# A fused audio tower on one core: idle products at both ends, w_out in four loads, down products that wait by chunk, and new orders of all engines

## The reference, cut to what matters

```
h  = (ln(x @ tok_W.T + tok_b)) * gamma + beta                  # tokenizer
h += attention0(ln(h); w_qkv, w_gates, w_out)                  # 16 heads of 64, softcap 50, causal, gated
h += tanh(ln(h) @ W @ A1 @ A2 + bias)                          # three weights in a row
h += attention1(ln(h); W_qkv, b_qkv, W_proj, b_proj)           # 16 heads of 16, Fenwick mask
h += fp4(silu(fp4(ln(h)) @ fp4(w_gate).T) * (fp4(ln(h)) @ fp4(w_up).T)) @ fp4(w_down).T
```

## Time and profile before

| | |
|---|---|
| three runs | 333.19, 333.32, 334.2 us; median 333.32 |
| the profiled execution | 332.38 us, of which its span is 330.5 us |
| mean granted TensorE clock | 0.974 |
| instructions | 11754, of them 10244 on TensorE (products and weight loads) |
| DMA | 12.80 MB |

### The profile page before, as it was taken

The page is one execution under the profiler, slowest core; times in us unless marked ns, Lnnn a source line. Parts: engine busy times, 40 slices in busy tenths (PEclk is TensorE's granted clock), DMA queues, the critical chain, the costliest instruction groups (busy, mean ns, idle before and its releaser), DMA issues.

```text
span 330.5 us, 11754 instructions
## 1 busy us (share of the span) xinstructions
PE 302.5 (92%) x5122; PEld 266.2 (81%) x5122; DVE 243.9 (74%) x527; ACT 115.5 (35%) x259; POOL 28.7 (9%) x49
## 2 busy tenths in 40 slices
...
GB/s 238 368 344 195 1 3 131 2 2 2 63 4 5 4 2 2 2 3 2 20 3 20 2 4 0 2 4 4 17 3 20 2 2 3 4 2 0 2 0 63
DMA packets 8773, 12.80 MB, mean 39 GB/s; under 512 B 778, under 2 KB 5650, under 8 KB 8724
## 3 DMA queue, kind: packets, MB, share of 16 engines
q1 hardware_dynamic: 8724, 12.06, 11.0%
...
## 4 chain that ended last, share of the span: by engine, by line
PE 85%; DVE 5%; issue 4%; DMA 3%; ACT 1%; SPq 1%; POOLq 0%; POOL 0%; ACTq 0%; DVEq 0%
PE psum L1185 75%; PE psum L1364 2%; PE psum L1386 2%; DMA ffw_raw<-in_L_ffn_aux_weight_dram 2%; PE psum L1490 1%; PE psum L1270 1%; DMA tokw_raw<-in_L_tok_W_dram 1%; PE psum L1245 1%; PE psum L1201 1%; PE psum L1293 1%; ACT hTb L557 1%; DVE hha L820 0%; PE psum L1467 0%; POOLq L220 0%; SPq L472 0%
## 5 line engine op out<-in xcount | busy, mean ns | idle before, releaser
L542 POOL TENSOR_TENSOR ln_rs<-ln_mv,minus_half 128x1 f32<-128x1 f32 x40 | 27.6, 692 | 267.5 <-DVE ln_mv L876 267.5
L1185 PE MATMUL psum<-aT_hi,wqkv_hi 128*128 128x256 f32 x128 | 38.0, 297 | 0.2
L1185 PE MATMUL psum<-aT_lo,wqkv_hi 128*128 128x256 f32 x128 | 36.9, 288 | 0.0
L1185 PE MATMUL psum<-aT_hi,wqkv_lo 128*128 128x256 f32 x128 | 36.6, 286 | 0.0
L557 ACT ACTIVATE qkT<-psum 128x512 f32<-128x512 f32 x32 | 19.1, 598 | 41.8 <-PE psum L1185 41.8
L1185 PE MATMUL psum<-wout_s,oT 128*128 128x256 f32 x128 | 29.2, 381 | 0.0
L1185 PEld LDWEIGHTS psum<-wout_s,oT 128*128 128x128 f32 x128 | 23.9, 190 | 3.3 <-issue 0.2
L1185 PEld LDWEIGHTS psum<-aT_hi,wqkv_hi 128*128 128x128 f32 x128 | 25.0, 196 | 1.2 <-ACT qkT L557 0.3
L1185 PEld LDWEIGHTS psum<-aT_lo,wqkv_hi 128*128 128x128 f32 x128 | 24.9, 195 | 0.1
L1185 PEld LDWEIGHTS psum<-aT_hi,wqkv_lo 128*128 128x128 f32 x128 | 24.9, 195 | 0.0
L1185 PE MATMUL psum<-v_aug,probs 32*32 32x65 f32 x1024 | 19.2, 220 | 0.0
(11 more groups left out here) (222 smaller groups left out, 747.8 us busy)
## 6 DMA issues: line engine op xcount, KB each, us to landing
...
```

Of the source, the lines that this page charges most:

```text
L542: nc.gpsimd.tensor_tensor(ln_rs[:, s, k, j:j + 1], ln_mv[:, s, k, j, 1:2], minus_half[:, :], ALU.pow).then_inc(rstd_ready[f"{k}_{j}"], 1)
L1185: return nc.tensor.matmul(o_, a, b, start=first, stop=last)
```

## The change

1. Ten steps `warm0` to `warm9` in the `pe` list: each waits for the constants and multiplies the identity by 320 columns of the constants into `att` bank 2, where nothing reads it. Two stand ahead of `turn_tok`, one ahead of `xT0.0`, two ahead of `bcast`, five between `tok1.0` and `xT0.1`. Four steps `tail0` to `tail3` do the same into the bank of `out1.3`; one stands ahead of `down_1.3`, three behind it.
2. `wout` loads w_out in four DMAs of 256 KB; ahead of the second to fourth SyncE waits until the one before has landed. `out_` waits for all four.
3. `down` waits for the copy of `hT0` ahead of chunk 0 and for that of `hT1` ahead of chunk 4.
4. All five lists are new.

```diff
@@ sync: wout
             def wout(i):
                 prep.made(sp, 0, "ffwT", "c1T", "ffc")
-                load_w("wout", wout_s[:, :, :], w_out.rearrange("(c p) n -> p c n", p=P))
+
+                n = INNER // P // WOUT_PIECES
+                for k in range(WOUT_PIECES):
+                    if k:
+                        sp.wait_ge(ld["wout"], 16 * k)
+                    load_w("wout", wout_s[:, k * n:(k + 1) * n, :],
+                           w_out[k * n * P:(k + 1) * n * P, :].rearrange("(c p) n -> p c n", p=P))
@@ tensor
+            def warm(i):
+                pe.wait_ge(ld["consts"], 16)
+                mm(att[:, 2, 0:WARM], ident, cst[:, 0:WARM], True, True)
+
+            def tail(i):
+                ring1.read_out(pe, LAST, "out0", "out1")
+                mm(ring1.bank(LAST, "out1")[:, 0:WARM], ident, cst[:, 0:WARM], True, True)
@@ tensor: out_
-                        pe.wait_ge(ld["wout"], 16)
+                        pe.wait_ge(ld["wout"], 16 * WOUT_PIECES)
@@ tensor: down
-                    ring2(i).read_out(pe, i, f"hT0_{j}", f"hT1_{j}")
                     for c in range(FC):
+                        if c in (0, 4):
+                            ring2(i).read_out(pe, i, f"hT{c // 4}_{j}")
```

The starts of the lists, and the end of the `pe` list, before and after (the rest is new in the same way):

```diff
@@ ORDER["pe"], first and last steps
-        turn_tok xT0.0 bcast tok0.0 xT1.0 tok1.0 xT0.1 turn_ff tok0.1 xT1.1 join_ff1 aT.0 tok1.1 qk2.0 qk0.0
-        qk6.0 qk1.0 qk5.0 v02.0 qk7.0 qk3.0 v11.0 v12.0 qk4.0 v01.0 v00.0 v10.0 xT0.2 turn_gate1 aT.1 join_ff2
-        s00.0 s01.0 s10.0 turn_gate0 s11.0 mix00.0 qk7.1 qk3.1 qk5.1 mix01.0 mix02.0 qk4.1 qk0.1 qk6.1 qk1.1
-        mix10.0 v00.1 mix11.0 v02.1 v11.1 oT00.0 mix12.0 oT01.0 v01.1 v10.1 turn_up1 out0.0 turn_up0 v12.1
-        tok0.2 xT1.2 turn_down qk2.1 ...
-        ... u1_0.3 hT0_0.2 hT1_0.2 g0_1.3 g1_1.3 u0_1.3 hT0_1.2 u1_1.3 hT1_1.2 down_0.2 down_1.2 hT0_0.3 hT1_0.3
-        down_0.3 hT0_1.3 hT1_1.3 down_1.3
+        warm1 warm9 turn_tok warm0 xT0.0 warm3 warm6 bcast tok0.0 xT1.0 tok1.0 warm8 warm7 warm2 warm4 warm5
+        xT0.1 turn_ff aT.0 tok0.1 qk7.0 xT1.1 join_ff1 v01.0 v11.0 qk6.0 v10.0 v12.0 qk2.0 qk3.0 v00.0 qk4.0
+        qk5.0 qk0.0 qk1.0 tok1.1 v02.0 turn_gate0 s00.0 s01.0 join_ff2 s10.0 s11.0 mix00.0 turn_gate1 aT.1
+        xT0.2 mix01.0 mix02.0 qk4.1 qk3.1 qk5.1 qk0.1 v02.1 mix10.0 v10.1 qk1.1 qk7.1 qk6.1 qk2.1 oT00.0
+        turn_up0 oT01.0 mix11.0 mix12.0 v11.1 v00.1 v01.1 turn_down out0.0 ...
+        ... hT0_1.2 u1_0.3 hT1_1.2 hT0_0.2 down_1.2 yT_1.3 hT1_0.2 g0_1.3 g1_1.3 u0_1.3 u1_1.3 hT0_0.3 hT1_0.3
+        down_0.2 down_0.3 hT0_1.3 hT1_1.3 tail1 down_1.3 tail3 tail0 tail2
@@ ORDER["act"], first steps
-        turn_tok tables xT0.0 split_qkv1 bcast split_qkv2 xT1.0 split_qkv0 split_qkv4 xT0.1 ...
+        tables turn_tok xT0.0 split_qkv1 bcast xT1.0 split_b split_qkv5 split_qkv3 split_qkv2 xT0.1 split_qkv0
+        aT.0 split_qkv4 turn_ff xT1.1 ...
@@ ORDER["dve"], first and last steps
-        turn_tok xT0.0 split_tokb split_qkv1 tokA0.0 xT1.0 tokB0.0 tokC0.0 split_qkv0 st1_0.0 ln1_0.0 tokA1.0
-        tokB1.0 xT0.1 ... w1b turn_gate1 s0.0 w1c s1.0 turn_gate0 w1d w1e w2a w2b ...
-        ... hh_0.3 hc_1.3 hd_1.3 he_1.3 hf_1.3 hg_1.3 hh_1.3 down_0.2 down_1.2 down_0.3 down_1.3
+        split_tokb turn_tok xT0.0 split_qkv1 tokA0.0 tokB0.0 xT1.0 tokC0.0 st1_0.0 split_b tokA1.0 ln1_0.0
+        tokB1.0 tokC1.0 st1_1.0 split_qkv3 ln1_1.0 xT0.1 split_qkv5 aT.0 tokA0.1 tokB0.1 split_qkv4 xT1.1 w0a
+        ... w2a s0.0 ln1_0.1 turn_gate0 st1_1.1 ln1_1.1 s1.0 w1c aT.1 xT0.2 mixA0.0 w2b mixB0.0 w1d w1e w1f
+        mixC0.0 w2c w1g turn_gate1 w1h w2d w2e w2f w2g turn_up0 w2h mixA1.0 mixB1.0 mixC1.0 out0.0 ...
+        ... sa0_1.3 hh_0.3 sa1_1.3 sb0_1.3 sb1_1.3 ha_1.3 ... hh_1.3 down_0.2 down_0.3 down_1.2 down_1.3
@@ ORDER["sp"]
-        load.2 wout load.3 store_0.0 store_1.0 store_0.1 store_1.1 store_0.2 store_1.2 store_0.3 store_1.3
+        load.2 wout load.3 store_1.0 store_0.0 store_0.1 store_1.1 store_0.2 store_0.3 store_1.2 store_1.3
```

More of the change, by code:

```diff
@@ L35 @@
 SLOTS = 3
+WOUT_PIECES = 4
+WARM = 320
 QKVG = 3 * INNER + H0
@@ L51 @@
[L51 to L65, removed]
@@ L66 @@
-        u1_0.3 hT0_0.2 hT1_0.2 g0_1.3 g1_1.3 u0_1.3 hT0_1.2 u1_1.3 hT1_1.2 down_0.2 down_1.2 hT0_0.3 hT1_0.3
-        down_0.3 hT0_1.3 hT1_1.3 down_1.3""",
-    "act": """
[L69 to L84, removed]
@@ L85 @@
-    "dve": """
-        turn_tok xT0.0 split_tokb split_qkv1 tokA0.0 xT1.0 tokB0.0 tokC0.0 split_qkv0 st1_0.0 ln1_0.0 tokA1.0
[L87 to L110, removed]
-        ya_1.2 sa1_0.2 yb_1.2 sb1_0.2 yc_1.2 yd_1.2 turn1_1.3 ye_1.2 sb0_0.2 yf_1.2 ha_0.2 yg_1.2 den1_0.3
-        yh_1.2 max1_1.3 norm1_0.3 sub1_1.3 yT_1.2 hb_0.2 back1_1.3 hc_0.2 sa0_1.2 proj_0.3 hd_0.2 st4_0.3
-        he_0.2 sa1_1.2 yn_0.3 den1_1.3 ya_0.3 norm1_1.3 hf_0.2 yb_0.3 sb1_1.2 sb0_1.2 yc_0.3 proj_1.3 yd_0.3
-        st4_1.3 ye_0.3 hg_0.2 yf_0.3 yn_1.3 yg_0.3 ya_1.3 yh_0.3 yb_1.3 ha_1.2 yT_0.3 yc_1.3 hb_1.2 yd_1.3
-        hc_1.2 hh_0.2 ye_1.3 hd_1.2 yf_1.3 sa0_0.3 he_1.2 yg_1.3 sa1_0.3 yh_1.3 hf_1.2 sb0_0.3 yT_1.3 hg_1.2
-        sb1_0.3 ha_0.3 hh_1.2 hb_0.3 sa0_1.3 hc_0.3 sb0_1.3 hd_0.3 sa1_1.3 he_0.3 sb1_1.3 hf_0.3 ha_1.3 hg_0.3
-        hb_1.3 hh_0.3 hc_1.3 hd_1.3 he_1.3 hf_1.3 hg_1.3 hh_1.3 down_0.2 down_1.2 down_0.3 down_1.3""",
```

78 lines of the change are left out of this document (71 added, 7 removed).

## The result

| | before | after |
|---|---|---|
| median (lowest to highest), 11 runs each | 333.32 (331.44 to 334.54) us | 329.33 (325.65 to 332.58) us |
| the profiled execution | 332.38 us, span 330.5 | 330.09 us, span 328.2 |
| mean granted TensorE clock in it | 0.974 | 0.984 |

The ratio is 0.9853, with a 95% interval of 0.9811 to 0.9895: 3.5 to 6.3 us faster. It leaves out the changed kernel's three slowest executions (330.68, 330.76 and 332.58 us), which the medians of the table count; by these medians the ratio is 0.988. The two profiled executions differ by only 2.3 us, since the one before lies 0.94 us under its median and the one after 0.76 us over it; terms read from the traces add up to 2.3, not to the 4.0 between the medians.

The account below looks back on a forecast made before the run. From 62 to 282.4 us TensorE's work bounds the kernel, at the end VectorE's chain. 3.9 + 0.6 - 1.0 + 1.0 = 4.5 us off 332.38 gives 327.9, plus 0.94 to the median: 328.8 us, range 323.5 to 332.5.

Parts of the forecast that it names:

- the likeliest case: Whole kernel: the forecast itself holds, 326.5 to 331 us, chance 0.61.
- A: Scores near 53 us: w_out in four loads shortens the stall, join_ff2 fills a wait, clock holds; 3.9 us gained (0 to 5.5).
- B: Start and first stage: idle products keep the clock up, VectorE's list sets qk7.0's start; 0.6 us gained (-1.0 to 2.5).
- C: Quantised weights, w1c to w2h: TensorE arrives sooner, turn_down waits 1 us for VectorE; -1.0 us (0 to -2).
- D: The end: hT0_1.3's lateness goes, down waits by chunk, tail1 costs 0.6 us without cover; 1.0 us gained (0.3 to 2.5).
- E: All other moves: 2.1 us to win in the full stretch, as much easily lost; 0 us (-2 to 2).
- The rival that the split does nothing: Scores: fetch late for another reason, stall and half clock stay; A 0.7, sum 1.3, 332.0 us; chance 0.12.
- the prediction's walk through VectorE's list: First stage and quantised weights: step durations added up, putting qk7.0's start at 23 us and w2h's end at 77.2.
- the 4 us at which the prediction called itself wrong: Between 62 and 282 us: TensorE's idle time passing 4 us was a sign that the prediction is wrong.
- The slower rival: Behind w_out's four loads: a second block also late by 2.06 us, clock falls; sum -1.5, 334.8 us; chance 0.07.
- the rival in which more is won: Whole kernel: no fetch late beside 256 KB, VectorE in time; 9.5 us gained, 323.8 us; chance 0.20.

Follow-up runs that it names:

- first group: Follow-ups on w_out's load and the idle products; its two variants of the kernel before: four loads alone, 331.10 us, and one load issued later, 329.28 us.
- the late one: Kernel before, its one w_out load issued only when the first values product of attention0 is made: 329.28 us, ratio 0.9879.
- the late load: Changed kernel with w_out in one load, issued when mix02.0 has been made: 328.39 us, ratio 0.984; profiled execution 325.57 us.

## Why the prediction was right, point by point

The forecast was 328.8 us; 329.33 was measured, within the range and within the likeliest case's own. By its terms (us gained, from the two profiled executions):

| term | forecast | found |
|---|---|---|
| A, w_out and `join_ff2` | 3.9 | 4.9 (2.0 of idle time, 2.9 of clock) |
| B, start | 0.6 | 0.0 |
| C, quantised weights | -1.0 | 0.0 |
| D, end | 1.0 | 2.5, of it 1.0 as forecast |
| E, other moves | 0 | -5.1 (3.4 of idle time, 1.7 of clock) |
| sum | 4.5 | 2.3 |

The idle times are those of the stretches above. Of the clock, 3.4 us at half (119.4 to 122.8) cost at most 1.7; A's 2.9 is what the sum then needs. A reading of its own comes from two kernels of the first group: from the first product of `s10.0` (51.09 before, 51.80 with four loads, 50.91 with the late one) to the copy (90.17, 87.25, 85.50) they take 3.6 and 4.5 us less, of which 1.1 and 1.9 are the stall and 2.5 and 2.6 the clock. The forecast had 2.3 for it. The late load alone in the kernel before, stall and clock together, gave 1.21% or 4.0 us where A's forecast had 0.9 + 2.3 for the two.

**A** was right in mechanism and in size. The stall came down to 0.25 + 0.62 us, where 1.2 was taken. Beside four loads the same block is still late by some 0.8 us more than with none (0.96 for 0.15), so moving the load away does fully what splitting it does in part. The rival that the split does nothing is out. So is what the prediction read from the rule beside it. The Trainium skill (DMA: Bandwidth & Descriptors, Queues, rings and completion order) has each engine take its queues in turn by packets, by which 16 KB would pass whatever the load's size. The three stalls of 2.06, 0.96 and 0.15 us say that here size and moment of the load count. No trace tells whether the engines kept to that rule while the block waited to start.

**B**: the first step behind `join_ff1` started at 27.55 us, where 26.9 was forecast; `qk7.0` came at 23.95 for 23, behind an idle 1.42 us ahead of `aT.0`. The profile ascribes that to "issue", but two other rows end it:

```profile
19.71 1.42 POOL L552 TENSOR_TENSOR ln_rs<-ln_mv,minus_half 128x1 f32<-128x1 f32 x1 [1.43 <-DVE ln_mv L886]
...
21.17 0.41 DVE L891 TENSOR_SCALAR n<-res,ln_mv,ln_rs 128x256 f32<-128x256 f32 x1 [0.44 <-POOL ln_rs L552]
```

`aT.0` starts at 21.69, 0.11 us after VectorE has made its input `n`, and VectorE had waited 0.44 us for GpSimd, which the prediction's walk through VectorE's list left out. The term mixed two large numbers that cancel: in the new order the warms are worth 3.3 us, and without them the changed kernel stands 2 us behind the old one at that step (29.51 for 27.55). That the idle products are no gain by themselves the kernel before shows: 2% slower with them.

**C**: VectorE ended w2h at 76.2 us, not 77.2, and TensorE came at 76.85. What was off is the walk through VectorE's list, by 1.0 us, in the safe direction.

**D**: VectorE's last step to the end of the span fell from 8.12 to 7.12 us: the 0.7 and 0.3 of the forecast, the latter measured by itself, 0.3. Another 1.5 us came from VectorE's list ahead of that, which the range had and the sum had not.

**E** is the step that failed. "As much is easily lost" named it and priced it at 0 (-2 to 2): idle time from 62 to 282.4 us rose by 3.4 us to 5.55, past the 4 us at which the prediction called itself wrong. 2.5 of the rise are the stalls at 113.20 and 119.32; in the two traces without them the idle time there is 3.05 us. The slower rival had a second late block, but beside w_out's loads, and made the loads its cause. The late block came 60 us behind them with no load there. So the total was met because a larger A and a larger end paid for it: right in its main term, lucky in its sum. With the block in time one execution took 325.57 us (the late load), over halfway to the rival in which more is won; another, which paid 2.81 us beside its one load, took 329.50.
